# Indirect transfers and weighted sums by half batches, one power for two batches in the last norm, and a new order

## The reference

```
x = layernorm(x + attention0(x))     # 16 heads of 8, causal, no biases
x = layernorm(x + moe0(x))           # 8 experts, top 2, hidden 256, relu
x = layernorm(x + attention1(x))     # 16 heads of 8, full, biases
x = layernorm(x + moe1(x))           # 15 experts, top 3, hidden 128, gelu gate, plus a shared expert of 256
layernorm(x) = (x - mean) / sqrt(var + 1e-5)
```

## Time and profile before

| | us |
|---|---|
| median of 3 runs | 1232.21 |
| lowest, highest | 1225.54, 1235.29 |
| the profiled execution, its span | 1241.11, 1239.3 |
| TensorE busy, weight loads | 963.7, 797.1 |
| VectorE, ScalarE, GpSimd busy | 671.0, 550.4, 445.5 |
| 160 scatters, 160 gathers on GpSimd | 155.9, 154.9 |

### The profile page before, as it was taken

The page is one execution under the profiler, slowest core; times in us unless marked ns, Lnnn a source line. Parts: engine busy times, 40 slices in busy tenths (PEclk is TensorE's granted clock), DMA queues, the critical chain, the costliest instruction groups (busy, mean ns, idle before and its releaser), DMA issues.

```text
span 1239.3 us, 22949 instructions
## 1 busy us (share of the span) xinstructions
PE 963.7 (78%) x7486; PEld 797.1 (64%) x7486; DVE 671.0 (54%) x2209; ACT 550.4 (44%) x1320; POOL 445.5 (36%) x695
## 2 busy tenths in 40 slices
PE   5899994968999778569998799686669827777840
PEld 4788883857999666457886576455448716656730
DVE  4476663644444557555556688654435603455643
ACT  1455652524655455346664577344356403222210
POOL 6010100254000644462005533554530370455565
PEclk9899997988999878889997899878879968888875
DMA  4666558343664233336853333322346935577312
GB/s 79 125 137 130 126 122 159 73 117 83 160 173 113 53 53 49 92 62 144 194 135 55 66 50 46 53 47 50 59 149 186 283 112 136 150 221 210 114 43 61
DMA packets 111510, 138.47 MB, mean 112 GB/s; under 512 B 12036, under 2 KB 85794, under 8 KB 111394
## 3 DMA queue, kind: packets, MB, share of 16 engines
q1 hardware_dynamic: 100002, 114.97, 41.2%
q0 software_dynamic: 10240, 20.99, 6.5%
q10 hardware_dynamic: 1152, 1.05, 0.5%
HBM read 70.25 MB, written 42.48 MB: 91 GB/s over the span
## 4 chain that ended last, share of the span: by engine, by line
PE 55%; another core or an unknown queue 14%; DMA 7%; issue 6%; DVE 6%; ACT 5%; SPq 4%; POOL 2%; ACTq 0%; DVEq 0%; POOLq 0%
PE bank_O L1112 7%; PE bank_N L1204 5%; PE bank_T L1090 5%; DMA QK<-parts 5%; PE bank_S L1063 4%; PE bank_FH L1192 4%; PE bank_S L1067 3%; ACT P L928 3%; PE bank_T L1094 3%; PE bank_S L1065 3%; PE bank_N L1120 2%; PE bank_T L1092 2%; PE bank_M L1036 2%; POOL G L871 2%
## 5 line engine op out<-in xcount | busy, mean ns | idle before, releaser
L1278 DVE TENSOR_REDUCE mp<-bank_S 128x3 f32<-128x384 f32 (+1 forms) x512 | 307.8, 619 | 211.0 <-PE bank_S L1067 95.9
L928 ACT ACTIVATE P<-bank_T 128x384 f32<-128x384 f32 (+1 forms) x512 | 259.3, 543 | 143.2 <-PE bank_T L1094 56.1
L871 POOL DMA_INDIRECT G<-yd,ypos x160 | 154.9, 968 | 136.2 <-issue 43.9
L855 POOL DMA_INDIRECT xs<-X,ypos x160 | 155.9, 975 | 51.4 <-issue 49.9
L1112 PE MATMUL bank_O<-P,V 128*32 128x256 f32 (+1 forms) x2048 | 137.8, 391 | 22.7 <-ACT OT L935 17.5
L1063 PE MATMUL bank_S<-QK 96*128 96x256 f32 x512 | 120.3, 334 | 18.5 <-DVE mp L1278 14.5
L1090 PE MATMUL bank_T<-QK 128*128 128x256 f32 x512 | 117.3, 334 | 16.9 <-ACT P L928 14.5
L1065 PE MATMUL bank_S<-rmat 128*128 128x256 f32 x256 | 92.6, 362 | 32.7 <-DMA QK<-parts 26.4
L1063 PEld LDWEIGHTS bank_S<-QK 96*128 96x128 f32 x512 | 85.7, 213 | 34.7 <-DVE mp L1278 24.7
L1090 PEld LDWEIGHTS bank_T<-QK 128*128 128x128 f32 x512 | 83.6, 211 | 35.3 <-ACT P L928 25.1
L1067 PE MATMUL bank_S<-QK 96*128 96x128 f32 (+1 forms) x512 | 104.8, 292 | 0.0
(11 more groups left out here) (170 smaller groups left out, 1797.7 us busy)
## 6 DMA issues: line engine op xcount, KB each, us to landing
QK<-parts SPq DMA_DIRECT2D x192, 128.0 KB
QK<-wtab SPq DMA_DIRECT2D x76, 257.0 KB
W<-w_in SPq DMA_DIRECT2D x46, 321.0 KB
QK<-xs SPq DMA_DIRECT2D x38, 256.0 KB
yd<-P SPq DMA_DIRECT2D x38, 256.0 KB
xs<-zeros SPq DMA_DIRECT2D x17, 512.0 KB, 7.7
xp<-xs SPq DMA_DIRECT2D x22, 256.0 KB
yd<-yb SPq DMA_DIRECT2D x22, 256.0 KB, 4.2
```

What stands on the lines that cost most here:

```text
L855: pool.indirect_dma_start(xs[g % 2], bass.IndirectOffsetOnAxis(ypos[L][:, 2 * b + blk, k:k + 1], 0), X[:, 2 * b + blk, :], None).then_inc( ...
L871: pool.indirect_dma_start(G[i][:, blk, k, :], None, yd[g], bass.IndirectOffsetOnAxis(ypos[L][:, 2 * b + blk, k:k + 1], 0))\
L928: act.activation(P[:, (h // 4) % 2, h % 4, 0:n], bank[("T0", "T1")[h % 2]][:, 0:n], ACT.Exp, scale=SCALE)\
L1278: dve.tensor_reduce(mp[:, a % 2, 0:n, h], bank[("S0", "S1")[h % 2]][:, 0:n * w] .rearrange("p (a c) -> p a c", a=n), AX.X, ALU.max).then_i ...
```

## The change

Scatter, gather and combine become steps of half a batch (`blk`), each with a due time of its own; the planner takes 1.26 us for a transfer where it took 1.23. Gather waits for the same half of the weighted sum two batches before, and each half of a slot has its own semaphore. The last norm's power is done for an even batch together with the following odd one, except for the last two batches, which stay single. All constants in `PRM` are new. The arithmetic per element is the same.

```diff
+def power_batches(q):
+    return 1 if q >= 2 * NB - 2 else 2 * (q % 2)
...
-       "period": (26.14, 21.28, 22.15), "first": (8.98, 7.51, 12.53, 12.66), "lag_s": (6.48, 8.09, 9.84, 7.91),
+       "period": (39.26, 50.01, 174.33), "first": (11.97, 27.51, 6.8, 100.51), "lag_s": (7.45, 17.14, 45.5, 34.76),
...
-       "scat": (141.84, 127.95), "xT": 174.08, "norm": (41.71, 3.29), "qk": (3.99, 360.99, 3.84),
+       "scat": (249.41, 166.78), "xT": 106.28, "norm": (174.79, 35.9), "qk": (1.39, 400.0, 134.56),
...
-       "wait": (0.03, 0.02, 0.23, 1.22, 0.21), "pe": 1.06, "qk1": (8.91, 240.89, 3.43), "max1": (1.19, 1.18, 6.72),
+       "wait": (0.02, 0.05, 0.09, 0.06, 0.25), "pe": 1.12, "qk1": (7.05, 400.0, 1.61), "max1": (0.0, 14.67, 10.31),
...
+        if not last or power_batches(q):
+            add(t + PRM["norm"][0], "POOL", 0.76 if last else 1.4, 0.1, "inverse_std", kind, q, after=[("stats", kind, q)])
+        add(t + PRM["norm"][1], "DVE" if last else "ACT", 0.5 if last else 0.9, 0.1, "normalise", kind, q,
+            after=[("inverse_std", kind, q + 1 if last and not power_batches(q) else q)])
...
-            add(t + PRM["scat"][0] + PRM["scat"][1] * TOPK[L] * i, "POOL", 2.46 * TOPK[L], 2.5, "scatter", q0 + i,
-                after=[("ypos_add", q0 + i), ("normalise", 0, q0 + i), ("clear_xs", filled[-1])] + read)
+            for blk in range(2):
+                add(t + PRM["scat"][0] + PRM["scat"][1] * TOPK[L] * (i + blk / 2), "POOL", 1.26 * TOPK[L], 2.5, "scatter", q0 + i, blk,
+                    after=[("ypos_add", q0 + i), ("normalise", 0, q0 + i), ("clear_xs", filled[-1])] + read)
...
-            add(due_combine + gap * i, "POOL", 2.46 * TOPK[L], 2.4, "gather", q,
-                after=[("page_store", c) for c in first] + [("ypos_add", q), ("combine", q - RC)])
+            for blk in range(2):
+                t = due_combine + gap * (i + blk / 2)
+                add(t, "POOL", 1.26 * TOPK[L], 2.4, "gather", q, blk,
+                    after=[("page_store", c) for c in first] + [("ypos_add", q), ("combine", q - RC, blk)])
+                add(t + PRM["comb"], "DVE", (0.6, 0.88)[L], 0.1, "combine", q, blk,
+                    after=[("gather", q, blk), ("route_weight", q)] + ([("shared_add", q - NB)] if L else []))
...
+                    n = power_batches(q)
                     pool.wait_ge(var_ready.sem, var_ready.all(q - NB))
-                    pool.tensor_tensor(r[:, 1, :], r[:, 0, :], half[:, 0, :], ALU.pow).then_inc(powered[k].sem, 4)
+                    if n == 2:
+                        r = rstd[:, k, q - 1:q + 1, :, :]
+                        pool.tensor_tensor(r[:, :, 1, :], r[:, :, 0, :], half[:, 0:1, :].broadcast_to((D, 2, 2)), ALU.pow)\
+                            .then_inc(powered[k].sem, 8)
+                    else:
+                        pool.tensor_tensor(r[:, 1, :], r[:, 0, :], half[:, 0, :], ALU.pow).then_inc(powered[k].sem, 4)
...
+                for k in range(TOPK[L]):
+                    pool.indirect_dma_start(xs[g % 2], bass.IndirectOffsetOnAxis(ypos[L][:, 2 * b + blk, k:k + 1], 0),
+                                            X[:, 2 * b + blk, :], None).then_inc(scattered[g].sem, DMA)
...
-                    pool.wait_ge(combined[L].sem, combined[L].all(b - RC))
+                    pool.wait_ge(combined[L].sem, combined[L].at(b - RC, TOPK[L] * (blk + 1)))
...
+                dve.wait_ge(gathered[L][i][blk].sem, gathered[L][i][blk].all(b // RC))
+                if blk == 0:
+                    dve.wait_ge(weighted[L].sem, weighted[L].all(b))
+                    dve.wait_ge(normed[0].sem, normed[0].all(q))
+                    if L == 1:
+                        dve.wait_ge(sh_added.sem, sh_added.all(b))
+                t = X[:, 2 * b + blk, :]
                 for k in range(TOPK[L]):
+                    if k:
+                        dve.wait_ge(sig.sem, sig.at(b, TOPK[L] * blk + k))
+                    dve.scalar_tensor_tensor(out=t, in0=G[i][:, blk, k, :], scalar=wk[L][:, b, blk, k:k + 1], in1=t,
+                                             op0=ALU.mult, op1=ALU.add).then_inc(sig.sem, 1)
```

More of the change, by code:

```diff
@@ L177, in norm @@
         add(t, "DVE", 0.85 if last else 0.73, 0.1, "stats", kind, q, after=after)
-        add(t + PRM["norm"][0], "POOL", 0.76 if last else 1.4, 0.1, "inverse_std", kind, q, after=[("stats", kind, q)])
-        add(t + PRM["norm"][1], "DVE" if last else "ACT", 0.5 if last else 0.9, 0.1, "normalise", kind, q, after=[("inverse_std", kind, q)])
+        if not last or power_batches(q):
+            add(t + PRM["norm"][0], "POOL", 0.76 if last else 1.4, 0.1, "inverse_std", kind, q, after=[("stats", kind, q)])
+        add(t + PRM["norm"][1], "DVE" if last else "ACT", 0.5 if last else 0.9, 0.1, "normalise", kind, q,
+            after=[("inverse_std", kind, q + 1 if last and not power_batches(q) else q)])
     def attention(a, t):
@@ L256, in chunk @@
         C0 = (0, C1_FROM)[L]
-        add(t - PRM["pre"][L], "SP", 0.48, PRM["l_x"][L], "x_load", c, after=[("scatter", q) for q in range(2 * NB) if group_of(q) == g]
+        add(t - PRM["pre"][L], "SP", 0.48, PRM["l_x"][L], "x_load", c, after=[("scatter", q, 1) for q in range(2 * NB) if group_of(q) == g]
             + [("page_T", n) for n in chunk_pages(c - rx)[-1:] if c >= C0 + rx] + ([("scores_T", NA - 2, 15)] if L else []))
@@ L286, in shared @@
         add(t + 4.2, "DVE", 0.44, 0.1, "shared_add", b,
-            after=[("shared_fc2", b)] + [("scatter", q) for q in range(2 * NB) if group_of(q) == group_of(NB + b)],
+            after=[("shared_fc2", b)] + [("scatter", q, 1) for q in range(2 * NB) if group_of(q) == group_of(NB + b)],
             frees=shared_y_bank(b))
@@ L306, in group @@
             q = q0 + i
-            add(due_combine + gap * i, "POOL", 2.46 * TOPK[L], 2.4, "gather", q,
-                after=[("page_store", c) for c in first] + [("ypos_add", q), ("combine", q - RC)])
-            add(due_combine + gap * i + 6.0, "DVE", (1.42, 2.12)[L], 0.1, "combine", q,
-                after=[("gather", q), ("route_weight", q)] + ([("shared_add", q - NB)] if L else []))
-            norm(1, q, due_combine + gap * i + 7.5, [("combine", q)])
+            for blk in range(2):
[4 more added lines that the diff above has]
+                    after=[("gather", q, blk), ("route_weight", q)] + ([("shared_add", q - NB)] if L else []))
+            norm(1, q, due_combine + gap * (i + 0.5) + PRM["comb"] + 1.5, [("combine", q, 0), ("combine", q, 1)])
             if L:
@@ L619, in build @@
         y_stored = [[signal(f"y_stored{L}{i}", DMA) for i in range((RY, RY1)[L])] for L in range(2)]
-        gathered = [[signal(f"gathered{L}{i}", 2 * TOPK[L] * DMA) for i in range(RC)] for L in range(2)]
+        gathered = [[[signal(f"gathered{L}{i}{c}", TOPK[L] * DMA) for c in range(2)] for i in range(RC)] for L in range(2)]
         combined = [signal(f"combined{L}", 2 * TOPK[L]) for L in range(2)]
@@ L852, in scatter, with gather @@
                 pool.wait_ge(normed[0].sem, normed[0].all(a))
-                for blk in range(2):
-                    for k in range(TOPK[L]):
-                        pool.indirect_dma_start(xs[g % 2], bass.IndirectOffsetOnAxis(ypos[L][:, 2 * b + blk, k:k + 1], 0),
-                                                X[:, 2 * b + blk, :], None).then_inc(scattered[g].sem, DMA)
-            def gather(q):
+                for k in range(TOPK[L]):
+                    pool.indirect_dma_start(xs[g % 2], bass.IndirectOffsetOnAxis(ypos[L][:, 2 * b + blk, k:k + 1], 0),
+                                            X[:, 2 * b + blk, :], None).then_inc(scattered[g].sem, DMA)
+            def gather(q, blk):
                 L, b = q // NB, q % NB
                 g = group_of(q)
-                if b == GROUP[g][1]:
+                if b == GROUP[g][1] and blk == 0:
                     wait_stored(pool, g)
```

40 lines of the change are left out of this document (14 added, 26 removed), and 11 rows, old and new, of the table PRM.

## The result

Against the forecast of 1205 us the changed kernel takes 1234.6 us (median of 14 runs, 1231.0 to 1248.2) beside 1230.5 for the kernel before on the same chip (14 runs, 1219.0 to 1238.3): ratio 1.0056, 95% interval 1.0029 to 1.0083. That is within 1% of no change, a loss of half a per cent rather than the gain of 2% I had given the largest chance. Ratios leave out runs more than 1.5% above the fastest of their kernel (one of order_only's four, at 1473.9 us, is the only far one) and are not the ratio of the medians, so where the two differ I give both; here the medians alone would say 1.0033.

The account below looks back on a forecast made before the run. Bounds: long runs of indirect transfers on GpSimd, beside which other engines do less, then GpSimd's queue at the end. Terms -10 - 14 - 2 - 1 = -27 us, from 1232 to 1205 us; range 1178 to 1247.

Parts of the forecast that it names:

- What bounds the kernel: Long runs of GpSimd's indirect transfers, beside which other engines do less; at the program's end, GpSimd's own queue.
- Scatters by halves: Scatters on GpSimd: shorter runs of transfers give TensorE time back; 10 us saved, half of a costed 20.
- seams: Places between two half scatters on GpSimd; half were taken as likely to have nothing between them, so 20 us became 10.
- Gathers and sums by halves: From 1060 us on, GpSimd's gathers wait for half a weighted sum, not a whole one; 14 us saved.
- Powers: Last norm on GpSimd: 16 powers become 9, a double one costing 0.72 to 1.43 us; 2 us saved.
- Last half: Program end: after the last gather lands, 3 sums instead of 6 remain; 0.8 us, entered as 1.
- New order: Every engine's queue is reordered by new planner priorities; put at 0, widening the range by 10 us either way.
- Slower by longer runs in layer 0: Layer 0's groups of 32 scatters each go as one run, 32 us lost together: 1250 us; chance 0.18.
- little: Halves issued back to back, sums staying behind the pages on VectorE; 8 us saved, 1224 us; chance 0.22.
- instruction fetches: Alternative reading of unexplained stops: sequencers' DMA fetches held up by traffic, making the 10 us from gaps 0.

Follow-up runs that it names:

- order_only: The kernel before with the changed kernel's constants and nothing else, on a chip without stops: 1126.2 us, 1.0526 of the kernel before.
- two_singles_after: The changed kernel with each double power replaced by two single ones, on a chip with stops: 1233.2 us, 1.0052 of the kernel before.
- before_again: The kernel before, unchanged, profiled a second time on a chip without stops: 1067.5 us.
- after_again: The changed kernel, run once more on a chip without stops: 1071.3 us, 1.0026 of the kernel before.
- few_scatters_after: The changed kernel with 12 instead of 36 scatters issued for the last group, chip without stops: 1070.4 us, 1.0020 of the kernel before.
- few_scatters_again: The kernel before with 12 instead of 36 scatters for the last group, chip without stops: 1066.3 us, 0.9992 of the kernel before.
- no_powers_before: The kernel before without the 16 powers of the last norm, on a chip with stops: 1225.6 us, 0.9986 of the kernel before.
- code_only: The changed kernel with the constants of the kernel before, on a chip without stops: 1117.8 us, 1.0454 of the kernel before.

## Why the forecast was wrong

In short: of the 27 us, the 10 from cut-up runs came to some 3 us of TensorE idle time, which did not reach the end of the attention, and the 14 from half sums came to nothing with halves alone; the new order shortens the gathers' stage, but starts it later and does more TensorE work before it.

**What bounds the kernel.** The stops are real and large, and the rows of the trace were read rightly: the longer the run of transfers, the less goes on. (The trace before has 23 separate runs of 4 and not six; in all of them TensorE is busy 82%, so the reading stands.) That is a correlation, and nothing that ran tests whether the length of a run is the cause. What I could not see is that the stops belong to the chip. The kernel before takes 164 us less where they do not occur, and the change is no gain in either case.

**Scatters by halves, -10.** This step failed first, and not at the seams. Up to 940 us the change does cut the runs up: counted with up to 0.9 us between two transfers there are 51 where there were 38, none over 10 where two were of 12. But TensorE's idle time inside them is 58.7 and 61.4 us in the two profiles of the new order (after, two_singles_after), against 60.5 to 67.3 in five of the old: some 3 us less, not 10. Most of the new runs are of 2 and 3, with TensorE at 81 to 83%, but six are of 8 to 10, where there had been one of 8, and in these it is at 58 to 61%. All its idle time up to the last attention falls by some 6 us (151 against 153 to 161), and its busy time for the same matmuls grows by as much (780 and 784 us against 773 to 779), so nothing is left of it. The last run goes the other way, from 30 transfers to 33. The last attention ends at 931.0 and 935.5 us in the two profiles of the new order, at 934.5, 932.0, 933.0, 931.3 and 932.4 in five of the old: nothing won. After it, compare the stretch from the last attention to the first gather, first in the kernel before and the changed one with stops (before, then after):

```profile
934.50:1060.00 125.50, 88.52 (x534) 78.04 (x535) 49.58 (x148) 45.37 (x104) 38.73 (x49) 0.86 0.65 190
```

```profile
931.00:1060.00 129.00, 93.63 (x569) 82.51 (x566) 53.01 (x162) 45.90 (x113) 39.10 (x51) 0.85 0.65 197
```

and without stops (before_again, then after_again):

```profile
834.60:924.30 89.70, 86.10 (x551) 77.99 (x552) 50.83 (x152) 47.16 (x107) 39.30 (x50) 1.00 0.88 264
```

```profile
835.90:929.00 93.10, 89.53 (x572) 79.95 (x573) 53.58 (x164) 45.69 (x114) 39.38 (x51) 1.00 0.88 276
```

The stretch is TensorE's work for the pages plus its idle time: 3.6 us of idle without stops, 35 to 37 with them, in both kernels. In these four traces its length does not follow where in it the scatters lie. The changed kernel scatters 24 us sooner in the traces with stops and 17 without (906 against 923) and gets nothing. Without stops that is because the pages decide (few_scatters_after, few_scatters_again); with stops TensorE is idle as long, only earlier. It also has 3 to 5 us more TensorE work in this stretch in both pairs, and is 3.5 us longer there. This repeats: the stretch takes 129.0 and 129.9 us in the two profiles of the new order with stops, 125.2 to 127.1 in five of the old, with 35.4 to 37.0 us of idle time in all seven; without stops 93.1 and 94.7 against 89.7 and 90.0.

**Gathers and sums by halves, -14.** The saving that I priced, the end of a half sum, did not come. I took the sum's end as what the gathers wait for and halved it. On chips with stops VectorE does not begin a sum until the run of gathers is over, and its page step comes first; the period goes from 10.98 to 10.88 us with halves alone. On chips without stops there was nothing to halve: gathers go back to back, waiting 0.3 us in all for sums (before_again) and 1.8 (after_again). The price I left out is the order of the sums: three that depend on each other take 1.12 us, where six in alternation took 1.66, 11.5 us of VectorE in all. In the changed kernel's own order this stage is shorter all the same. From the first group's first gather to the last group's first it takes 101.6 us in both profiles with stops, against 108.9 to 113.6 in five of the old order; its waits for sums are no less in total (33.1 and 29.8 us against 33.0), so the gain is of the new order with the halves, not of the halves alone. It begins some 4 us later (1060 and 1065 against 1057 to 1060), which leaves the 5 us of lead noted above, and the medians do not show that this reaches the end.

On chips without stops the stages can be added up, two profiles of each kernel: the first gather comes 3.0 us later (929 and 926 against 924 and 925), from there to the last group's first gather it takes 79.2 us instead of 81.3, and from there to the end 0.3 us less. That is 0.6 us in all: what the stage wins, about what the double powers save, is less than the later start costs.

**Powers, -2.** The double power costs 1.02 us, inside my bounds of 0.72 to 1.43, and saves 14 x 0.72 - 7.1 = 3.0 us of GpSimd's queue. An effect on the time of that size is below what two_singles_after and no_powers_before resolve.

**Last half, -1.** In the trace after, the last gathers are summed in threes with 1.6 to 2.7 us of waiting before each; no run isolates this term, and it would be below what they resolve.

**New order, 0 with 10 either way.** Not separable, as order_only and code_only show.

**The rivals.** "Slower by longer runs in layer 0" did not come: its runs are 10 at most. The measured case is nearest to "little" (1224), yet on the other side of the kernel before. What I had no case for was the plain one: the waits I counted had other waits or moved work behind them, so that shortening a stage started the next no sooner.

**What stays open**: which part makes the 0.5%. Halves alone in the old order have ratios of 1.0041 and 1.0045, so they can account for it; halves with the old order of sums have 1.0037, not told apart from that. On chips with stops the profiled executions of the new order are on the whole the shorter ones and the medians the longer ones, and where the other executions lose the 5 us of lead is not known. Nor is it known whether a gap, fewer scatters or another engine's issuing avoids the stops. No version that does all the work beats the kernel before.

## What to carry to other kernels

Before a wait is given a price, take the waiting work away altogether and see whether the time moves: leaving out 16 powers showed in one run that at most half a per cent was to be had from them, and leaving out 24 scatters that nothing was to be had there on chips without stops. Such a run counts for the kind of chip it ran on: the same omission was never run where the stops are, which is where the forecast wanted its 10 us. Look too at what stands in one queue behind a wait: the changed kernel's last page stores stand behind a load that waits for scatters they have no need of. Splitting a step wins only if its first half can start earlier on the engine that does it, so look at what that engine does, and what stands first in its queue, at the moment the half is ready. The constants of a planner go with the steps they order (old code with new constants 1.0526, new code with old ones 1.0454); here code and constants could not be costed one by one.

## What the chips showed that I had not expected

The same program takes 1230 us on some chips and 1067 on others. Of the 174 us between the spans of before and before_again, TensorE's busy time for the same 7486 matmuls makes 53.5 (963.7 against 910.2, at a mean granted clock of 0.88 against 0.93) and its idle time 120. Of these 120, 68 lie inside GpSimd's runs of indirect transfers (137 against 69) and 46 more in the 3 us behind each run. In the first 240 us, before the first transfer, the two traces are alike (TensorE busy 199.8 and 201.2 us). In these 20 us of the run of scatters the DMA queues moved (packets, MB, share of the time of 16 engines), first with stops, then without:

```profile
q0 software_dynamic: 516, 1.05, 15.0%
q1 hardware_dynamic: 144, 0.26, 5.5%
```

```profile
q1 hardware_dynamic: 3305, 4.63, 80.1%
q0 software_dynamic: 525, 1.06, 13.9%
q8 instruction: 1, 0.02, 0.3%
q14 instruction: 2, 0.02, 0.2%
```

GpSimd's own queue q0 moves the same in both; SyncE's q1 nearly stands still with the stops, as TensorE, VectorE and ScalarE do. The Trainium skill, "DMA: Bandwidth & Descriptors", section "SWDGE vs HWDGE vs iDMA", says that DMAs with hardware-made descriptors are immune to the interference by which VectorE can hold up GpSimd's descriptor writing; whatever stops the chip here is another thing or more than that, since it reaches q1 (5.5% against 80.1%) and engines that issue no DMA. The instruction fetches that I weighed in the forecast do not explain this stop either: in the trace with stops no packet of the instruction queues lies between 998 and 1018 us, nor beside the restart at 1017 to 1018 us. The cause was not found.
